# A graph network kernel: the one-column GpSimd operation ahead of each group of message scatters is replaced by a bare semaphore increment

## The reference, cut to what matters

```python
msgs = edge_val[:, None] * x[edge_col]                       # 200,000 messages of 256 values
agg = jax.ops.segment_sum(msgs, edge_row, num_segments=6250) # edge_row is `src`, edge_col is `dst`
x = _layernorm(x + relu(agg @ W.T))                          # the first layer
x = _layernorm(x + second_layer(x, src, dst, ...))           # kron products, attention, a GRU, a last linear
```

## Time and profile before

| what | value |
|---|---|
| median of three timed runs | 9202.79 us (9187.38 to 9215.10) |
| the profiled execution, its own time | 9201.89 us |
| its span in the profile | 9200.4 us |
| busy in the span | PE 6627.9, PE's weight load 4195.6, DVE 5809.9, ACT 3779.0, POOL 4407.1 us |
| mean granted clock of TensorE | 0.867 |
| message stage, from POOL's first `gate` to its last scatter | 904.9 to 3056.7 us |

### The profile page before, as it was taken

The page is one execution under the profiler, slowest core; times in us unless marked ns, Lnnn a source line. Parts: engine busy times, 40 slices in busy tenths (PEclk is TensorE's granted clock), DMA queues, the critical chain, the costliest instruction groups (busy, mean ns, idle before and its releaser), DMA issues.

```text
span 9200.4 us, 169831 instructions
## 1 busy us (share of the span) xinstructions
PE 6627.9 (72%) x32823; PEld 4195.6 (46%) x32824; DVE 5809.9 (63%) x16380; ACT 3779.0 (41%) x10923; POOL 4407.1 (48%) x4743
## 2 busy tenths in 40 slices
PE   3253666666666799988877777777777777777898
PEld 2122444444444577733334444444444444444444
DVE  8895444444443566644447777777777777776666
ACT  0000444444444100023336666666666666665333
POOL 0001777777778200000037776776666766674100
PEclk9676777777777999965569999999999999999988
DMA  0002333333322588844467777777777777776200
GB/s 12 0 0 79 100 100 99 99 101 99 99 97 96 194 262 263 262 186 197 192 208 210 205 205 203 204 203 205 200 205 199 207 202 204 203 204 175 64 19 18
DMA packets 973127, 1398.89 MB, mean 152 GB/s; under 512 B 378559, under 2 KB 744498, under 8 KB 959902
## 3 DMA queue, kind: packets, MB, share of 16 engines
q1 hardware_dynamic: 761663, 797.51, 29.0%
q0 software_dynamic: 208448, 596.38, 22.9%
q10 hardware_dynamic: 2586, 1.37, 0.1%
HBM read 986.18 MB, written 415.51 MB: 152 GB/s over the span
## 4 chain that ended last, share of the span: by engine, by line
PE 32%; issue 18%; DVE 16%; DMA 13%; SPq 8%; ACT 7%; POOL 3%; DVEq 1%; ACTq 1%; POOLq 0%
DMA arena_n<-rec_dram 8%; PE ps L1993 7%; SPq L550 7%; PE ps L1890 4%; PE ps L1787 4%; ACT junk L1001 3%; DMA arena_e<-msg_dram 3%; PE ps L2011 3%; PE ps L2002 3%; POOL msg_dram L814 2%; PE ps L1905 2%; DVE arena_r L1305 2%; DVE arena_e L1636 2%; DVE arena_e L1576 2%; ACT L1022 1%
## 5 line engine op out<-in xcount | busy, mean ns | idle before, releaser
L835 POOL DMA_INDIRECT arena_n<-tab_dram,idxs x2624 | 2621.1, 999 | 2756.0 <-DVE idxs L1551 1667.7
L1993 PE MATMUL ps<-arena_n 126*128 126x257 f32 x5232 | 1635.3, 416 | 404.6 <-DVE arena_e L1576 370.3
L814 POOL DMA_INDIRECT msg_dram<-arena_e,idxq x1616 | 1625.6, 1006 | 434.4 <-issue 424.9
L1001 ACT ACTIVATE junk<-ps 128x256 f32<-128x256 f32 x2616 | 995.2, 382 | 1065.8 <-PE ps L1993 937.5
L1879 PE MATMUL ps<-arena_n,arena_r 128*128 x3232 | 1085.1, 494 | 352.9 <-ACT arena_r L902 352.9
L1993 PEld LDWEIGHTS ps<-arena_n 126*128 126x128 f32 x5232 | 868.9, 196 | 910.1 <-DVE arena_e L1576 735.4
L1576 DVE COPY arena_e<-ps 128x257 f32<-128x257 f32 x1962 | 816.5, 422 | 681.7 <-ACT junk L1001 672.9
L1636 DVE SCALAR_TENSOR_TENSOR arena_e<-arena_e,rstd,nbetak_b 128x256 f32<-128x256 f32 x2608 | 1087.4, 481 | 31.6 <-ACT arena_e L1008 18.9
L1879 PEld LDWEIGHTS ps<-arena_n,arena_r 128*128 128x128 f32 x3232 | 753.6, 245 | 592.6 <-issue 466.2
L907 ACT ACTIVATE arena_e<-ps,recq 128x256 f32<-128x256 f32 x1616 | 736.7, 474 | 651.9 <-PE ps L1879 645.7
L1890 PE MATMUL ps<-arena_e,oh 128*128 128x256 f32 x3520 | 816.2, 387 | 88.8 <-DVE oh L1359 88.3
(11 more groups left out here) (335 smaller groups left out, 9115.5 us busy)
## 6 DMA issues: line engine op xcount, KB each, us to landing
arena_n<-m_dram SPq DMA_DIRECT2D x2624, 126.5 KB
arena_e<-msg_dram SPq DMA_DIRECT2D x441, 514.0 KB, 4.5
m_dram<-arena_e SPq DMA_DIRECT2D x49, 1413.5 KB, 4.9
m_dram<-arena_e SPq DMA_DIRECT2D x49, 1285.0 KB, 4.5
arena_n<-tab_dram,idxs POOLq DMA_INDIRECT x2624
hist_dram<-arena_r SPq DMA_DIRECT2D x163, 253.0 KB
arena_n<-rec_dram SPq DMA_DIRECT2D x1616, 2.0 KB
msg_dram<-arena_e,idxq POOLq DMA_INDIRECT x1616
```

What stands on the lines that cost most here:

```text
L814: nc.gpsimd.indirect_dma_start(out=msg_dram, in_=msgs[:, u, j, :], in_offset=None, out_offset=bass.IndirectOffsetOnAxis(ap=idxq[:, u, j:j ...
L835: nc.gpsimd.indirect_dma_start(out=feat[:, u, i, :], out_offset=None, in_=tab_dram, in_offset=bass.IndirectOffsetOnAxis(ap=idxs[:, u, i:i ...
L1001: nc.scalar.activation(junk[:, i % 2, 0:D], ps[:, bank_of(i), 1:HC], ACT.Square, scale=1.0 / 16, accum_out=var[:, u % 2, i:i + 1]).then_in ...
L1993: mm(ps[:, bank_of(i), 0:HC], prods_t[0:KM, s % 2, j * P:(j + 1) * P], m_ring[0:KM, i, :], start=True, stop=True).then_inc(e_h, 1)
```

## The change

In POOL's loop over the message groups, the operation of one column is removed. The increment of `m_gate`, which was attached to it, becomes an instruction of its own behind the two waits. Nothing else is touched: the waits, the scatters, DVE's wait on `m_gate` and the buffer `gate` are as they were.

```diff
@@ -809,7 +809,7 @@
                 for u in range(4):
                     pool.wait_ge(m_loc, nth(it * 4 + u))
                     pool.wait_ge(m_msg, nth((it * 4 + u) * 4 + 3, HEAD))
-                    nc.gpsimd.tensor_tensor(gate[:, u:u + 1], ones[:, 0:1], ones[:, 1:2], ALU.mult).then_inc(m_gate, 1)
+                    pool.sem_inc(m_gate, 1)
                     for j in range(G):
                         nc.gpsimd.indirect_dma_start(
                             out=msg_dram, in_=msgs[:, u, j, :], in_offset=None,
```

## The result

| | kernel before | changed kernel |
|---|---|---|
| timed in the first series, median | 9202.03 us | 9120.02 us (9114.68 to 9127.72), ratio 0.9912, interval 0.9894 to 0.9929 |
| timed again in a later series | 9200.19 us | 9130.58 us (9124.80 to 9135.92), ratio 0.9927, interval 0.9908 to 0.9946 |
| span in the profile | 9200.4 us | 9113.4 us |
| first scatter starts, last scatter ends | 905.7, 3056.7 us | 906.9, 2979.1 us |
| the message stage between the two | 2151.0 us | 2072.2 us |

The kernel is 0.7 to 0.9% faster, 70 to 82 us. The forecast was 9140, so 62 us. Of the 87.0 us by which the two profiled spans differ, 78.8 are in the message stage. The rest, 8 us net, lies mostly in the last stage by tiles. No code differs there, and that stage has 704 to 718 us in the profiles of this study; the changed kernel itself has 704 in its first profile and 717 in its later one.

The account below looks back on a forecast made before the run. POOL was taken to bound the message stage. Pause 33.5 + first scatter 6.5 + collisions 21.6 = 61.6 us, taken from the profiled 9201.9, gave 9140 us; the forecast's own range was 9122 to 9160.

Parts of the forecast that it names:

- The bound: Message stage: POOL is the bound, and each 0.01 us taken from a group's cycle is worth 4 us.
- The pause: Between groups on POOL: without the gate, 0.388 us shrinks to 0.305, 403 times, winning 33.5 us.
- The first scatter: Each group's first scatter on POOL falls from 1.000 us to the others' 0.984, winning 6.5 us.
- all medians are 984 ns: Sign in the new profile's message stage: all scatters of a group have a median of 984 ns.
- Collisions: Third scatters held up by DVE's one-hot: 44 of 57 long ones gone at 0.49 us each, 21.6 us won.
- part 3: Scatters shifting against DVE's one-hot; on the far side, some five one-hots nearing the fourth scatter, 1 to 2 us neglected.
- The increment at zero: The increment of `m_gate` standing by itself on POOL's sequencer costs zero while the message margin covers it.
- part 2: The increment done by POOL's sequencer costs nothing; wrong if a group's first scatter has waits on ACT.
- Rival D: Cold start on POOL: each group's first scatter has 0.63 us instead of 0.39, 97 us more, 9299; chance 0.04.
- A: Only the pause is won: DVE shifts with the scatters, long cases stay, 40 us won, 9162; chance 0.15.
- B: No gain: waits and increment aren't hidden, the boundary between groups stays at 0.39 us, 9202; chance 0.10.
- C: More collisions: the flight gets shorter relative to the scatters, some 200 groups long instead of 57, 9232; chance 0.06.

Follow-up runs that it names:

- Experiments 1: Changed kernel with a one-column product put back on POOL behind the increment in every fourth group: 9138.5 us, ratio 0.9927 to the kernel before.
- 3: Changed kernel with a one-column memset, which reads nothing, on POOL behind the increment in every group: 9141.5 us, ratio 0.9930 to the kernel before.
- 4: Changed kernel with a copy of one SBUF column on POOL behind the increment in every group: 9205.6 us, ratio 1.0008 to the kernel before.
- experiment 2: Kernel before with a second one-column product on POOL behind the first in every group: 9340.0 us, ratio 1.0143 to the kernel before.
- Experiment 6: Kernel before with one more small DVE operation ahead of each group's one-hot: 9210.9 us, ratio 1.0013 (11276.7 us on the chip with 11157 for the kernel before).
- 7: Changed kernel with four more small DVE operations ahead of each one-hot: 9193.7 us, ratio 0.9991 to the kernel before (11278.9 us on the 11157 us chip).
- experiment 5: Changed kernel with four more bare increments of an unused semaphore on POOL in every group: 9115.6 us, ratio 0.9906 to the kernel before.
- experiments 8: Kernel before with DVE starting group g only when group g-2's scatters have landed: 11814.1 us, one execution, on the chip with 11157 us for the kernel before.
- 9: Changed kernel with DVE starting group g only when group g-2's scatters have landed: 11808.2 us, one execution, on the chip with 11157 for the kernel before.

## Why the prediction was right, point by point

- **The bound.** POOL, with 0.01 us a group worth 4 us: it held. A second gate lengthened the stage by its boundary and its collisions and no more, and a chain made longer by four operations on DVE cost the stage next to nothing but collisions. The margins shrank by more than the 0.6 us of the prediction: behind the first fifty groups the tightest one had its last message 3.5 us ahead of its first scatter before, and 1.7 after. That was still enough.
- **The pause, 33.5 us.** Measured 155.7 - 122.9 = 32.8 us. The small difference is a misreading: the boundary of the kernel before is 0.386 us over all groups, not 0.388. The row of the edge stage was the right one to take the price from; 0.305 us came out to the nanosecond.
- **The first scatter, 6.5 us.** This is the term that was mis-sized. Scatters got shorter in all four places and not in the first alone: 404 x 0.028 + 1212 x 0.0115 = 25 us. The prediction's sign "all medians are 984 ns" did not come: they are 972. I had taken 0.984 us as the natural length of this scatter because three of four had it. Experiments 1, 3 and 4 show that this was already the disturbed one; 0.972 is the natural one (0.976 in the later profile of the changed kernel). That the three later scatters of a group stood at 0.984 because of an operation up to four instructions back was not to be seen in a trace in which every group had the gate.
- **Collisions, 21.6 us.** 57 long third scatters became 12, and one fourth scatter is long besides; their excess fell by 21 us. The mechanism is right, and the near match of the number is luck. The limit fell to 1.82 us and not to 1.84, since two shorter scatters stand in front of the third and the boundary, where the prediction counted one; of the 57 cases only 11 lie under 1.84 (13 in the prediction) and 6 at 1.82 or below. The changed kernel then had more short flights, 12. Its later profile has 14 over 1.2 us and 16 short stalls besides. The reading that all other groups have a longer flight was wrong too: six are shorter, 1.45 to 1.61 us, with short stalls instead of long ones. The mechanism is shown by experiments 2, 6 and 7, with numbers that rise and fall as the shift asks. One sentence of part 3 was poor: the far side isn't harmless. Only one group, not five, stood beyond 0.79 us, but the crowd of one-hots 0.5 us behind the third scatter was in my rows and not in my count. It lies at the same distance in the changed kernel, short of the 0.79 us from which the fourth scatter is hit, because a scatter's end sets it: there DVE does shift with the scatters. Experiment 6 shows what one small operation more on DVE does to it.
- **The increment at zero.** Shown by experiment 5, and by the 0.305 us at each boundary. The prediction's sign against part 2, first scatters that wait for ACT, did appear in the list of waits, 118 times, but with 0.30 us each it shows no wait. Rival D is wrong while there is a margin. Without one, experiments 8 and 9 show what the bare increment costs more than the gate, 0.07 us.
- **The rivals.** A (9162) falls with the collisions' fall and with the flight that stayed, B with the pause. C needed the shift to go the other way; experiment 2 is C's shift made real, with 116 more collisions.
- **The sum.** 32.8 + 25.4 + 21.3 = 79.5 us against 78.8 of the stage; the pauses within the groups, 0.8 us longer in sum, make the difference. The 21.3 are what is left of the scatters' 46.7 us when the medians' 25.4 are taken off. The forecast was 61.6, and the mis-sized term accounts for the gap, 25.4 instead of 6.5. The time of the first series, 9120.02, lies 2 us below the forecast's own range of 9122 to 9160; that of the later series, 9131, lies inside. The stage came out at 2072 us and not at about 2090, and the mean scatter at 977 ns and not at about 990, for the same reason.

## What to carry to other kernels

When an engine is the bound and runs a rigid pattern, price a removed operation by the distance between its neighbours with and without it, not by its duration: 0.217 us of gate were worth 0.081 us of boundary. Then look at what the shorter pattern shifts: two engines with a short exclusion repeat their phase in every round, so 0.1 us of shift can win or lose as much as the operation. Look at both directions of the exclusion: an engine that is held until the other's end takes over its phase, and work added to it doesn't shift it by its own length. And take a price from a stage of the same kernel that already has the new form, if there is one.

## What the runs showed of the hardware that I had not expected

- A scatter of 128 rows on POOL takes 0.972 us (0.976 in one profile). Behind a lone operation of one column that reads SBUF the next two take 0.983 and 0.987; where every group has such an operation, all four take 0.982 to 1.000. Behind a memset, which only writes, they stay at 0.973.
- A memset of one column (0.126 us at the median) between two indirect DMAs is hidden in their 0.305 us pause; an operation that reads is not (0.356 us for a copy, 0.386 for the product), and a second product adds 0.137.
- A DVE operation with two SBUF inputs (the one-hot, 0.69 us) that starts 0.05 to 0.5 us ahead of a scatter lets it end about 1.55 us after the one-hot's own start, whichever scatter it is: 1.50, 1.27 or 1.47 us long at 0.05, 0.28 and 0.07 us of lead. In the ten profiles with 9200 us for the kernel before, no scatter with a lead in that range went free. The Trainium skill's "SBUF — State Buffer", section "Who interferes with whom", holds that such an operation contends only with GpSimd's reads and infers that descriptor generation is not among them; the measurement shows that an indirect scatter is held up by it, at its start. Which part of the scatter's work is held up isn't shown. By the same page the first to start keeps the pair for its whole instruction; here a one-hot that starts 0.52 us into a scatter runs in its normal 0.69 us.
- A small DVE operation with one SBUF input (a copy, a cast or a product with a constant, about 0.17 us alone) that starts 0.52 to 0.79 us into a scatter of 0.98 us lasts until the scatter ends, 305 times of 305 in the kernel before. One that starts 0.20 to 0.50 us into it takes 0.21 us at most, 470 of them.
